# Node degrees counted in the edge scatter of a four-layer graph network instead of in the pass for the maximum

## The reference, cut to what matters

```
L0  h = leaky(concat(x[dst], edge_attr) @ w1 + b1) @ w2 + b2 ; summed by src ; update MLP
L1  e = leaky_relu(s_src[src] + s_dst[dst]) ; m = segment_max(e, dst)
    alpha = softmax over the edges of a destination ; coef = rel_table[edge_type] * alpha
    out = segment_sum(coef * z[src], dst)
L2  deg = segment_sum(ones, col) over the edges and one more loop per node
    norm = rsqrt(deg)[row] * rsqrt(deg)[col] ; out = segment_sum(h[row] * norm, col) + b ; mish
L3  agg = segment_sum(x[src], dst) / max(segment_sum(ones, dst), 1)
    h = x @ W_self.T + b_self + agg @ W_neigh.T + b_neigh ; relu
```

## Time and profile before

| | us |
|---|---|
| median of 3 runs | 3945.95 |
| lowest and highest | 3945.78, 3947.28 |
| the profiled execution, its own time | 3951.51 |
| its span | 3949.8 |
| busy in it: TensorE (matmul) | 2757.8 |
| VectorE | 2593.6 |
| GpSimd | 2025.6 |
| ScalarE | 1608.0 |

### The profile page before, as it was taken

The page is one execution under the profiler, slowest core; times in us unless marked ns, Lnnn a source line. Parts: engine busy times, 40 slices in busy tenths (PEclk is TensorE's granted clock), DMA queues, the critical chain, the costliest instruction groups (busy, mean ns, idle before and its releaser), DMA issues. The chain is left out here.

```text
span 3949.8 us, 88026 instructions
## 1 busy us (share of the span) xinstructions
PE 2757.8 (70%) x19674; PEld 2007.0 (51%) x19675; DVE 2593.6 (66%) x7923; ACT 1608.0 (41%) x4084; POOL 2025.6 (51%) x2354
## 2 busy tenths in 40 slices
PE   2314555445455545988888888888898967769599
PEld 2213333333334334888888888888884232234345
DVE  8724555555555555988888888888895669940501
ACT  1001222222222223777777777777774523220201
POOL 0016666666666667888888888888880000000100
PEclk9955666765665577999999999999998979979797
DMA  9972222222222213777777777777774658848082
GB/s 385 414 314 63 65 64 65 62 64 63 66 65 64 65 56 109 208 209 209 210 209 209 209 209 209 209 208 210 208 212 178 249 216 293 290 158 316 8 332 99
DMA packets 702423, 696.70 MB, mean 176 GB/s; under 512 B 51182, under 2 KB 633536, under 8 KB 692640
## 3 DMA queue, kind: packets, MB, share of 16 engines
q1 hardware_dynamic: 672386, 636.28, 51.6%
q0 software_dynamic: 25792, 54.52, 4.1%
q10 hardware_dynamic: 4190, 5.22, 0.4%
HBM read 340.91 MB, written 354.90 MB: 176 GB/s over the span
## 5 line engine op out<-in xcount | busy, mean ns | idle before, releaser
L893 POOL DMA_INDIRECT sorted_rows<-rows,posi x806 | 782.5, 971 | 556.2 <-issue 324.2
L1173 DVE SCALAR_TENSOR_TENSOR acc<-acc,keep,pm 128x256 f32<-128x256 f32 x1504 | 717.8, 477 | 155.2 <-DMA count_matrices<-acc 96.0
L841 PE MATMUL s_peq<-sb_w1bb,eT 128*128 128x256 f32 x806 | 388.1, 582 | 560.2 <-ACT eT L708 456.0
L1004 POOL TENSOR_SCALAR ohs_e<-iota,rt 128x128 f32<-128x128 f32 x1128 | 672.7, 611 | 11.4 <-DMA rt<-sorted_rows 11.4
L1100 PE MATMUL pm<-ohw_e,ohs_e 128*128 128x128 f32 x3008 | 662.7, 302 | 0.0
L1013 POOL TENSOR_TENSOR hid<-pre_e,excess 128x512 f32<-128x512 f32 x376 | 533.5, 1419 | 223.0 <-ACT excess L1040 223.0
L1106 PE MATMUL px<-PN,dT 128*128 x4512 | 498.6, 219 | 0.2 <-ACT dT L1047 0.2
L841 PEld LDWEIGHTS s_peq<-sb_w1bb,eT 128*128 128x128 f32 x806 | 188.3, 286 | 606.7 <-ACT eT L708 476.9
L1056 ACT ACTIVATE ohw_e<-ohd_e,rt 128x128 f32<-128x128 bf16 x1504 | 474.6, 386 | 0.0
L1100 PEld LDWEIGHTS pm<-ohw_e,ohs_e 128*128 128x128 f32 x3008 | 459.7, 193 | 0.0
L1099 PE MATMUL pm<-ohd_e,ohs_e 128*128 128x128 bf16 x1504 | 334.3, 222 | 153.6 <-DVE acc L1173 137.3
(11 more groups left out here) (299 smaller groups left out, 4479.3 us busy)
## 6 DMA issues: line engine op xcount, KB each, us to landing
count_matrices<-acc SPq DMA_DIRECT2D x1504, 128.0 KB, 2.1
ab<-count_matrices SPq DMA_DIRECT2D x75, 1600.0 KB, 7.9
sorted_rows<-zrow SPq DMA_DIRECT2D x188, 528.0 KB, 10.4
rt<-sorted_rows SPq DMA_DIRECT2D x376, 264.0 KB, 3.1
arb<-count_matrices SPq DMA_DIRECT2D x25, 1664.0 KB, 6.8
arb<-count_matrices SPq DMA_DIRECT2D x25, 1536.0 KB, 6.5
ef<-in_edge_attr_dram SPq DMA_DIRECT2D x58, 364.0 KB
sorted_rows<-rows,posi POOLq DMA_INDIRECT x806
```

The costliest lines, as they stand in the source:

```text
L841: nc.tensor.matmul(pe_q[:, q % 2, 0:2 * D], eT[:, q % 2, :], w1bb[:], start=True, stop=True).then_inc(s_q, 1)
L893: pool.indirect_dma_start(sortd, bass.IndirectOffsetOnAxis(ap=posi[:, h, c:c + 1], axis=0), rows[:, h, c, :], None).then_inc(s_sc[h], 16)
L1004: last = nc.gpsimd.tensor_scalar(ohs[:, k % BUFS, j, :], iota128[:], rt[:, k, j, D + 1:D + 2], None, ALU.is_equal)
L1173: nc.vector.scalar_tensor_tensor(acc[:, k % SUMS, j, :], before, keep[:, at:at + 1] if isinstance(at, int) else keep[:, ds(at, 1)], pm[:, ...
```

## The change

Degrees are counted in the scatter. For each half VectorE copies the destinations' places to `loc` and makes a third one-hot, `ohL` (128 wide, 16-bit floats), in four pieces of 4, 3, 3 and 3 columns, which follow the relation lookups 1, 4, 7 and 10 (counted from 0). TensorE multiplies `ohL` of each of the 13 columns with `ohD` into 25 columns of `lk` that were free, ahead of the lookups and behind a new wait for `s_rel`. VectorE adds these 25 columns to `DEG`, which is cleared once at the start, behind its wait for `s_lk`. To make room, the throw-away tiles `junkW` and `junkR` become 16-bit. In the pass for the maximum TensorE's whole part goes, with its semaphore, SyncE's wait for it and VectorE's seven copies; in the next stage the 25 multiplications and the copy to `DEG` go.

```diff
@@ -592,10 +592,13 @@
+                LOW = {1: (0, 4), 4: (4, 7), 7: (7, 10), 10: (10, 13)}
+                loc = sb2("loc", [P, 2, CH])
+                ohL = sb2("ohL", [P, 2, CH, P], F16)
...
-                junkW = sb2("junkW", [P, CH, NREL])
-                junkR = sb2("junkR", [P, CH, P])
+                junkW = sb2("junkW", [P, CH, NREL], BF16)
+                junkR = sb2("junkR", [P, CH, P], BF16)
@@ -740,6 +743,7 @@
+                        nc.vector.tensor_copy(loc[:, h, :], lo[:, 0, c])
@@ -749,6 +753,10 @@
                         for c in range(CH):
                             last = nc.vector.scalar_tensor_tensor(junkW[:, c, :], iotar[:], typc[:, h, c:c + 1], relt[:],
                                                                   ALU.is_equal, ALU.mult, accum_out=relc[:, h, c:c + 1])
+                            if c in LOW:
+                                a, b = LOW[c]
+                                nc.vector.tensor_tensor(ohL[:, h, a:b, :], iota128[:].unsqueeze(1).to_broadcast([P, b - a, P]),
+                                                        loc[:, h, a:b].unsqueeze(2).to_broadcast([P, b - a, P]), ALU.is_equal)
@@ -768,6 +776,7 @@
                         dve.wait_ge(s_lk, n + 1)
+                        nc.vector.tensor_tensor(DEG[:], DEG[:], lk[:, CH * NT:(CH + 1) * NT], ALU.add)
@@ -778,6 +787,7 @@
+                    link(nc.vector.memset(DEG[:], 0.0))
@@ -825,6 +835,10 @@
                             pe.wait_ge(s_ot, n + 1)
                             if not first:
                                 pe.wait_ge(s_lc, 3 * n - 2)
+                            pe.wait_ge(s_rel, n + 1)
+                            for c in range(CH):
+                                nc.tensor.matmul(lk[:, CH * NT:(CH + 1) * NT], ohL[:, h, c, :], ohD[:, h, c, :],
+                                                 start=(c == 0), stop=(c == CH - 1), skip_group_check=True)
@@ -1514,7 +1526,6 @@
                             sp.wait_ge(s_un, ((i - 1) * R + r) * 2 + 2)
-                            sp.wait_ge(s_dg, ((i - 1) * R + r) * 2 + 2)
                             load(i * R + r, r)
@@ -1546,25 +1557,6 @@
-                    dve.wait_ge(s_dg, 2 * NT)
-                    for c, (a, b) in enumerate(CUTS):
-                        nc.vector.tensor_copy(DG[0:1, a:b], pg[:, c, 0:b - a])
-
-                @block.tensor
-                def _(pe):
-                    def step(i, first, final):
-                        for r in range(R):
-                            pe.wait_ge(s_ld[r], i * 16 + 16)
-                            for c, (a, b) in enumerate(CUTS):
-                                last = nc.tensor.matmul(pg[:, c, 0:b - a], ones[:, 0:1],
-                                                        ab[:, r, :, :].rearrange("p q d -> p (q d)")[:, a:b],
-                                                        start=first and r == 0, stop=final and r == R - 1,
-                                                        skip_group_check=True)
-                            last.then_inc(s_dg, 2)
...
@@ -1588,9 +1578,6 @@
-                    for t in range(NT):
-                        last = nc.tensor.matmul(pd[:, t:t + 1], DG[0:1, t * P:(t + 1) * P], ones[0:1, 0:1], start=True, stop=True)
-                    last.then_inc(s_d, 1)
@@ -1603,8 +1590,6 @@
-                    dve.wait_ge(s_d, 1)
-                    nc.vector.tensor_copy(DEG[:], pd[:, 0:NT])
```

More of the change, by code:

```diff
@@ L1499, in build @@
                 un = ctx.enter_context(nc.sbuf_tensor("un", [P, NT, P], F32))
-                pg = ctx.enter_context(nc.psum_tensor("m_pg", [1, len(CUTS), BANK], F32))
                 MXv = MX[:].rearrange("p (q d) -> p q d", q=NT)
@@ L1505, in build @@
                 s_mx = sem("m_max")
-                s_dg = sem("m_degree")
                 s_ago = sem("m_act_passed")
@@ L1548, in _ @@
                         step(s, False)
-                    dve.wait_ge(s_dg, 2 * NT)
-                    for c, (a, b) in enumerate(CUTS):
-                        nc.vector.tensor_copy(DG[0:1, a:b], pg[:, c, 0:b - a])
-                @block.tensor
-                def _(pe):
-                    def step(i, first, final):
-                        for r in range(R):
-                            pe.wait_ge(s_ld[r], i * 16 + 16)
-                            for c, (a, b) in enumerate(CUTS):
-                                last = nc.tensor.matmul(pg[:, c, 0:b - a], ones[:, 0:1],
-                                                        ab[:, r, :, :].rearrange("p q d -> p (q d)")[:, a:b],
-                                                        start=first and r == 0, stop=final and r == R - 1,
-                                                        skip_group_check=True)
-                            last.then_inc(s_dg, 2)
-                    step(0, True, False)
-                    with pe.Fori(1, NT // R - 1) as i:
-                        step(i, False, False)
-                    step(NT // R - 1, False, True)
             blocks.close()
@@ L1577, in build @@
                 tp = ctx.enter_context(nc.psum_tensor("x_tp", [P, 2, BANK], F32))
-                pd = ctx.enter_context(nc.psum_tensor("x_pd", [P, BANK], F32))
                 pr = ctx.enter_context(nc.psum_tensor("x_pr", [2 * NT, BANK], F32))
@@ L1581, in build @@
                 s_r = sem("x_reduced")
-                s_d = sem("x_degrees")
                 s_m = sem("x_rows")
```

## The result

The kernel after takes 3957.3 us (median of 7 runs, 3955.8 to 3960.2) where the kernel before takes 3945.8 (median of 7): the ratio is 1.0035, with a 95% interval from 1.0023 to 1.0046. It is slower, by 11.5 us or 0.35%, where 34 us were forecast. Its profiled execution took 3956.5 us, its span is 3954.8 us, 5.0 us more than that of before.

The account below looks back on a forecast made before the run. In the scatter no engine was near full, and gaps between GpSimd's DMA trains turned others' delays into time; TensorE bound the pass. 3951.5 - 53 + 87 = 3985.5 us profiled, so 3980 median; range 3900 to 4085.

Parts of the forecast that it names:

- The pass, -53 us: Pass for the maximum: without TensorE, VectorE's 50 minimums are the longest chain and `MX` transposes start 53 us sooner.
- rival D: Pass for the maximum: the loads bind it, gain 28 instead of 53 us, 4005; shares the forecast's chance of 0.53.
- TensorE's multiplications, 1.7 us per half: Scatter: 13 added multiplications ahead of the lookups, priced by the bin rows at 0.10 to 0.15 us each.
- VectorE's additions: Scatter, per half: add to `DEG` 0.2 us, copy to `loc` 0.1, four pieces 2.3.
- What of it shows, 1.4 us per half: Scatter: of 4.3 us added chain at most about 2.55 show beyond the slack; 1.4 taken, 87 us over 62 halves.
- slack: Scatter: VectorE's positions could come about 1.75 us later on average before delaying GpSimd's next train of 13 indirect DMAs.
- the mark that `positions` would be the last releaser of most trains: Scatter: line 759 (positions), no longer line 692 (ScalarE's projected rows), would last release most trains of DMAs.
- Rival C: Scatter: 26 more TensorE instructions bring the slowing sooner, trains pause before the ninth DMA; 3.3 us per half, 4098; chance 0.08.
- the stretched part: Scatter: second half of a DMA train, where the other three engines slow with no recorded wait; if it moves, prediction fails.
- Rival A: Scatter: pieces fill time in which VectorE stands anyway; 0.2 us per half, 3905, faster than before; chance 0.27.
- Rival B: Scatter: each of four pieces holds up an indirect DMA by 0.42 us; 104 us on top of the forecast, 4084; chance 0.12.
- The marks: Signs expected in the profile after: scatter period 21.7 us, wait for lookups 3.7 us per half, transposes 53 us sooner.

Follow-up runs that it names:

- e1: Kernel after without all counting of degrees (no `loc`, pieces, multiplications or add; degrees wrong): 3673.6 us, 0.986 of before on its chip.
- e6: Kernel before, with TensorE summing only the upper 16 bits of the counts in the pass for the maximum: 3682.0 us, 0.989 of before.
- e8: Kernel after with the 13 multiplications of each half made twice: 3676.1 us, 0.987 of before on its chip.
- r1: Kernel after, unchanged, on a chip where the kernel before takes 3724.4 us: 3675.8 us, 0.987 of before.
- e11: Kernel after without the pieces and `loc` copies in 60 of 62 halves, on a chip where before takes 3944.9 us: 3927.2 us, 0.995.
- e12: Kernel after without the 13 multiplications, the `s_rel` wait and the add, where before takes 3944.9 us: 3910.3 us, 0.992.
- r2: Kernel before, unchanged, run for its profile on the chip of r1: 3725.3 us.
- e7b: Kernel before, degrees taken as columns in the pass for the maximum, upper 16 bits of counts as weights, one PSUM clearing: 3668.6 us, 0.985 of before.

## Why the prediction was right or wrong

**The pass, -53 us: right.** 53.7 by the trace, 53.5 by e1. The loads kept up (rival D is out), and VectorE's idle time fell from 29.7 to 4.6 us because it had been waiting for buffers that TensorE held: in e6, which shortens TensorE's multiplications and changes nothing else, it is 4.6 us as well.

**TensorE's multiplications, 1.7 us per half: mis-sized.** Thirteen take 0.55 us at the half clock (808.12 above), and over all 62 halves their weights take 36.2 / 62 = 0.6 us. From the first weight load to the end of the thirteenth, 0.95 us pass on average; doubling them lengthens that by 0.35 us (1.13 in e8 against 0.78 in r1). I had taken the bin rows' 0.10 to 0.15 us, which move 128 columns each where these move 25. The nearest row was the wrong one in the one size that counts.

**VectorE's additions: right.** Pieces 146.4 / 62 = 2.36 us (2.3 forecast), the add 0.18 (0.2), the copy 0.17 (0.1).

**What of it shows, 1.4 us per half: too much by a third, and the step itself is wrong.** Measured were 1.04 us and 64.4 in all. The corrected chain is 0.6 + 0.2 + 0.2 + 2.36 = 3.3 us, less 1.75 of slack is 1.6; at the share that I took, 1.4 of 2.55, it is 0.87 us, 54 us in all, which would have given 3951.5 - 53 + 54 = 3953 against a profiled 3956.5 (with 0.95 us for the multiplications it would be some 67 us). So the mis-sized term carries the miss by the numbers. But that agreement is luck, for the step from chain and slack to time fails. By it, TensorE's part alone, 0.6 + 0.2 or at most 0.95 + 0.2 us, lies inside the slack of 1.75 and costs nothing; e11 measured 0.58 us per half. The pieces and the copy alone, 2.5 us, would have cost about 0.4 (0.55 of the excess); e12 measured 0.26. And the mark that `positions` would be the last releaser of most trains is wrong: in after ScalarE's rows end 66 of GpSimd's waits (257.4 us), `positions` 16 (21.5 us). What the runs show in place of the step: from before to after, GpSimd's waits for ScalarE's rows grew by 29.6 us (227.8 to 257.4, now in mid-train), its waits for the positions, the forecast's only road, by 17.6 (3.9 to 21.5), its other idle time by 13.2 and its DMAs by 4.5; together that is the 64.4 us within 0.5. And e11 shows that it is TensorE's part that puts the wait into the train. Why a hand-over is late there stays open. A small reading goes with it: of the 60 waits for the rows in before, 56 lie between trains and 4 inside one.

**Rival C: its pause happened, at a third of its price.** GpSimd waits for line 695 ahead of its ninth DMA, as C said, and e11 shows that TensorE's part is enough for it. C's own reason, that the slowing starts sooner with more work, is neither shown nor refuted. I had priced it at 3.3 us, as a pause on top of the gap. The traces show a pause in place of the gap: the train grew by 4.0 us and the gap shrank by 2.9. In these traces the stretched part limits itself: it ends when GpSimd stands still, wherever in a train that is.

**Rival A: right in its outcome on the other chips, and for the pieces on the first kind.** With no stretched part the change costs 0.09 us per half and the whole is 1.3% faster. I gave A 0.27 on the slack of one trace; that slack was itself a product of the stretched part, as the last sentence of the prediction warned. Where the stretched part exists, e12's 0.26 us per half is close to A's price of 0.2, and A's mechanism is seen there: the pieces fill pauses. What A had not reckoned with is TensorE's part.

**Rival B: real, but small with pieces this short.** The mean DMA went from 971 to 976 ns on the first chip, 4.5 us in sum where B had 104. B let every piece hold up a DMA by 0.42 us; in after 15 of the 248 pieces did so by the measure above, for 6.0 us together.

**The marks.** The period, forecast at 21.7 us, is 20.3 + 1.04 = 21.3. The wait for the lookups is 7.5 us per half, not 3.7, since the stretched part has moved there. Two terms were put at nothing. For the 16-bit throw-away tiles it holds on the faster chips: e1, with these tiles, has the scatter of r2, without them, within 0.1 us (on two chips of one kind). The new wait for `s_rel` is covered by TensorE's 22.5 us of idle time ahead of the new weights in after, 0.4 us per half at most. On a chip with the stretched part neither was run by itself.

## What to carry to other kernels

Where an engine waits with nothing recorded that it waits for, its slack isn't a property of the kernel: run the same kernel on another chip before you sell the slack. Price a matrix multiplication by a row with as few moving columns: at the half clock it was 0.15 us with 128 and 0.04 with 25 (0.55 / 13). With a single one (e7b, 25 in 0.83 us) it was 0.03, so below some 25 columns there was little left to gain. And before work is moved into a stage that is hard to read, ask whether it can be made cheap where it is: a narrower type for the same numbers gave the whole gain here and touched nothing else.

## What was unexpected of the hardware

The same kernel takes 3725 us on some chips and 3945 on others, steadily on each (all 6 or 7 runs of before in a group lie within 0.4%), and nearly all of the difference is in the one stage in which GpSimd issues indirect DMAs: the collecting stage behind it takes 1418 us on the first chip and 1417 on the other. On the slower kind all engines but GpSimd hand over late during the second half of a train, and come free together when GpSimd stops, 2.2 us after it in the lines above. TensorE's granted clock in the scatter is 0.65 there and 0.71 elsewhere, which may as well follow from its pauses as cause them. No run here shows the cause; it is open.

An indirect DMA that a VectorE comparison holds up ends 0.83 us behind it, whatever the comparison's length. One of 1.89 us made a DMA take up to 2.68 us instead of 0.96; of those of 0.55 to 0.68 us most did nothing. Work of that kind beside GpSimd's queue is cheap in short pieces.
